# A decoder block on Trainium2: all SiLUs ahead of the exponentials at the turn from projection to scan, the first relus on VectorE, and the thin passes in small sets

## The reference, cut to what matters

```python
z, xBC, dt_raw = split(layernorm(x) @ in_proj_w.T)          # 512, 640, 8 columns
xBC = silu(causal_conv4(xBC) + conv_b)                      # xs 512, B 64, C 64
dt  = softplus(dt_raw + dt_bias); dA = exp(dt * -exp(A_log))
h_t = h_(t-1) * dA_t + (dt_t * xs_t) B_t ;  y_t = h_t C_t   # 8 heads of 64, state 64
y   = rms((y + D * xs) * silu(z)) * ssm_norm_w @ out_proj_w.T
# then an MLP; then the mLSTM, whose gates are
gates = [q, k, v] @ gate_w + gate_b                         # k = v = ctx, 8 columns
```

## Time and profile before

| | us |
|---|---|
| median of 3 runs | 598.36 (597.4 to 600.65) |
| the profiled execution, its own time | 597.5 |
| its span, first to last instruction | 595.8 |
| TensorE busy | 563.0 (94%) |
| VectorE busy | 446.2 (75%) |
| ScalarE busy | 270.1 (45%) |
| GpSimd busy | 145.7 (24%) |

### The profile page before, as it was taken

How to read it: one execution, slowest core, us unless ns; L and a number is a source line. 1 busy time by engine, 2 the same in 40 slices (tenths; PEclk the granted TensorE clock), 3 DMA queues, 4 the chain that set the end, 5 groups by cost and what they waited for, 6 DMA issues and landing times. The chain is left out here.

```text
span 595.8 us, 9377 instructions
## 1 busy us (share of the span) xinstructions
PE 563.0 (94%) x2995; PEld 457.9 (77%) x2995; DVE 446.2 (75%) x990; ACT 270.1 (45%) x565; POOL 145.7 (24%) x209
## 2 busy tenths in 40 slices
PE   6989989999999899999999999999968999999995
PEld 5767666788898788888888888878854677777774
DVE  6996797399897324765755856587888999999994
ACT  2666778776787412311111112445524445444431
POOL 4130010144454121210110010007765122222200
PEclk9999999799999999999999999999958999999998
DMA  8300001000000092000000000011000000000000
GB/s 287 141 2 25 28 17 57 3 26 7 7 4 1 28 295 72 1 1 0 1 1 1 1 0 1 4 38 56 18 2 0 1 19 18 18 17 9 18 19 26
DMA packets 21392, 18.90 MB, mean 32 GB/s; under 512 B 12008, under 2 KB 20584, under 8 KB 20968
## 3 DMA queue, kind: packets, MB, share of 16 engines
q1 hardware_dynamic: 20920, 18.36, 9.7%
q10 hardware_dynamic: 432, 0.03, 0.1%
HBM read 16.04 MB, written 2.34 MB: 31 GB/s over the span
## 5 line engine op out<-in xcount | busy, mean ns | idle before, releaser
L926 PE MATMUL ps<-xnT,w_fc 128*128 128x256 f32 x512 | 112.8, 380 | 0.0
L926 PEld LDWEIGHTS ps<-xnT,w_fc 128*128 128x128 f32 x512 | 96.5, 190 | 12.7
L1662 PE MATMUL ps<-w_fc,scores 128*128 128x352 f32 x256 | 82.9, 479 | 2.4 <-ACT scores L1751 2.4
L1662 PEld LDWEIGHTS ps<-w_fc,scores 128*128 128x128 f32 x256 | 49.3, 198 | 30.1 <-ACT scores L1751 4.3
L1169 ACT ACTIVATE xs<-ps 128x512 f32<-128x512 f32 x32 | 19.1, 597 | 95.8 <-PE ps L926 75.7
L1282 DVE SCALAR_TENSOR_TENSOR fold<-xpad,conv_w,fold 128x256 f32<-128x256 f32 x120 | 50.9, 482 | 2.4 <-ACT fold L1071 1.6
L1681 PE MATMUL ps<-u_res,hT 128*128 128x256 f32 x192 | 45.9, 391 | 3.8 <-DVE scores L1860 2.8
L1681 PEld LDWEIGHTS ps<-u_res,hT 128*128 128x128 f32 x192 | 37.5, 196 | 11.8 <-issue 3.0
L809 PE MATMUL ps<-xnT,fold 128*128 128x256 f32 x160 | 37.7, 381 | 1.4 <-ACT xpad L1065 0.9
L809 PEld LDWEIGHTS ps<-xnT,fold 128*128 128x128 f32 x160 | 29.5, 190 | 8.4 <-issue 3.0
L735 POOL TENSOR_SCALAR q_ve<-q_mv 128x2 f32<-128x2 f32 x8 | 1.7, 218 | 129.3 <-DVE q_mv L1396 129.3
(11 more groups left out here) (299 smaller groups left out, 1207.4 us busy)
## 6 DMA issues: line engine op xcount, KB each, us to landing
zs<-in_ffn_w SPq DMA_DIRECT2D x1, 2112.0 KB, 11.1
x_res<-in_x SPq DMA_DIRECT2D x8, 256.0 KB, 7.9
w_fc<-in_w_fc SPq DMA_DIRECT2D x1, 2048.0 KB, 10.3
xnT<-in_ctxT SPq DMA_DIRECT2D x8, 256.0 KB, 3.1
xs<-in_ctx SPq DMA_DIRECT2D x16, 128.0 KB, 2.9
xs<-in_ctxT SPq DMA_DIRECT2D x8, 256.0 KB, 3.1
out<-scores SPq DMA_DIRECT2D x16, 128.0 KB, 1.7
fold<-in_w_in SPq DMA_DIRECT2D x2, 580.0 KB, 6.8
```

What stands on the lines that cost most here:

```text
L926: last = pe.matmul(bank[half + r][:, i * S:(i + 1) * S], m.w_fc1[:, kk, col:col + P], m.xnT[:, b, kk * S:(kk + 1) * S], start=(kk == 0), s ...
L1662: last = pe.matmul(bank[1 + j][:, 0:HALF], xT[:, p, k * P:(k + 1) * P], m.w_gu[:, k, j * HALF:(j + 1) * HALF], start=(k == 0), stop=(k == ...
```

## The change

1. **Taps.** ScalarE does the first tap of batches 0, 1 and 2 (`TAPPED = (0, 1, 2)`) instead of 6 and 7.
2. **Time passes.** `time_steps(j)` becomes `time_step(n)`, one tile at a time; the four of a step are put between other passes. `soft_start` waits for all 16.
3. **z passes first.** In steps 3 and 4 both z passes come before the next transposes (`ROWS_FIRST`).
4. **Context sums.** `ctx_sums` takes one batch: batches 0 to 4 in steps 5 to 9, batches 5 and 6 in step 10. One counter serves the context loads, each of which waits for the one before it.
5. **The turn.** On TensorE the z passes of batch 7 follow the two decay tiles of batch 0 one by one, and its second transpose of xs goes behind the first two `mix`. On ScalarE all SiLUs, those of z of batch 7 among them, come before the decay exponentials, and the exponentials of batches 0 and 1 follow. The four relus of batch 0 are done by VectorE (`first_exponents`).

```diff
...
     SCAN, MLP = 9, 18
     STEPS = MLP + B + 3
     PAD = CONV - 1
-    TAPPED = 6
+    TAPPED = (0, 1, 2)
+    ROWS_FIRST = (3, 4)
+    conv_steps = lambda b: sum(NCH * (PAD - 1 if i in TAPPED else PAD) for i in range(b))
+    taps_before = lambda b: NCH * sum(1 for i in TAPPED if i < b)
     ORDER = [4, 0, 1, 2, 3]
     PAIRS = KM // 2
     flat = lambda t: t.rearrange("p t h -> p (t h)")
...
     PAIR_OF_ONES = 1.0 + 0x3F80 * 2.0 ** -23
     PAIR_OF_MINUS_ONES = -(1.0 + 0xBF80 * 2.0 ** -23)
     CTX_SUMS = B - 1
-    CTX_FIRST = 3
+    CTX_STEP = 5
     CTX_AT = 3 * P
 
 
...
 
         def load_ctx(b):
             sp.wait_ge(s["z_ps"], C * (b + 1))
+            after(sp, g["ctx_in"], 16 * b)
             sp.dma_start(m.xnT[:, b, :].rearrange("p (k t) -> p k t", k=KD), m.a["ctxT"][:, :, b * S:(b + 1) * S])\
-              .then_inc(g["ctx_in0"] if b < CTX_FIRST else g["ctx_in1"] if b < CTX_SUMS else g["ctx_in2"], 16)
+              .then_inc(g["ctx_in"], 16)
 
         for b in range(4):
             load_ctx(b)
...
         def turned_u(b, kk):
             return m.xnT[:, b, kk * S:(kk + 1) * S]
 
-        def time_steps(j):
+        def time_step(n):
             pe.wait_ge(s["w_in_in"], 16 * KD)
-            pe.wait_ge(s["uT_ready"], 2 * j + 2)
-            for n in range(4 * j, 4 * j + 4):
-                for kk in range(KD):
-                    last = pe.matmul(bank[7][:, n * NH:(n + 1) * NH],
-                                     turned_u(n // C, kk)[:, (n % C) * P:(n % C + 1) * P],
-                                     w_in[:, kk, DIN - NH:DIN], start=(kk == 0), stop=(kk == KD - 1))
+            pe.wait_ge(s["uT_ready"], n // C + 1)
+            for kk in range(KD):
+                last = pe.matmul(bank[7][:, n * NH:(n + 1) * NH],
+                                 turned_u(n // C, kk)[:, (n % C) * P:(n % C + 1) * P],
+                                 w_in[:, kk, DIN - NH:DIN], start=(kk == 0), stop=(kk == KD - 1))
             last.then_inc(s["dt_ps"], 1)
 
         def sum_steps():
...
                 last = pe.transpose(bank[5][:, k * P:(k + 1) * P], xF[:, b % 2, k, c * P:(c + 1) * P], m.ident[:])
             last.then_inc(s["xsT_ps"], 1)
 
-        def ctx_sums(first, end, arrived):
-            pe.wait_ge(g[arrived], 16 * (end - first))
+        def ctx_sums(b, saved):
+            pe.wait_ge(g["ctx_in"], 16 * (b + 1))
             pe.wait_ge(s["weights_summed"], 1)
-            pe.wait_ge(s["g_saved"], B - 1)
-            for b in range(first, end):
-                for c in range(C):
-                    at = CTX_AT + (C * b + c) * 2 * XH
-                    for k in range(KD):
-                        pe.matmul(bank[6][:, at:at + 2 * XH], m.xnT[:, b, k * S + c * P:k * S + (c + 1) * P],
-                                  m.gate_kv[:, k, :], start=(k == 0), stop=(k == KD - 1))
+            pe.wait_ge(s["g_saved"], saved)
+            for c in range(C):
+                at = CTX_AT + (C * b + c) * 2 * XH
+                for k in range(KD):
+                    pe.matmul(bank[6][:, at:at + 2 * XH], m.xnT[:, b, k * S + c * P:k * S + (c + 1) * P],
+                              m.gate_kv[:, k, :], start=(k == 0), stop=(k == KD - 1))
 
         def ctx_sums_last():
-            pe.wait_ge(g["ctx_in2"], 16)
+            pe.wait_ge(g["ctx_in"], 16 * B)
             pe.wait_ge(s["decays_kept"], 1)
             for c in range(C):
                 for k in range(KD):
...
         for k in range(STEPS):
             b = k - SCAN
             if k < SCAN + 1:
+                tiles = range(4 * (k - 2), 4 * (k - 1)) if 2 <= k < 6 else None
                 on(channels, k - 2, [0, 1, 2])
-                if k == 3:
-                    rows(0, 0)
-                    rows(0, 1)
+                if tiles:
+                    time_step(tiles[0])
+                if k in ROWS_FIRST:
+                    rows(k - 3, 0)
+                    time_step(tiles[1])
+                    rows(k - 3, 1)
+                    time_step(tiles[2])
                 on(turn_u, 2 * k - 2)
-                if k > 3:
+                if k not in ROWS_FIRST:
                     on(rows, k - 3, 0)
+                    if tiles:
+                        time_step(tiles[1])
                 on(channels, k - 2, [3, 4])
+                if tiles and k not in ROWS_FIRST:
+                    time_step(tiles[2])
+                if k >= CTX_STEP:
+                    ctx_sums(k - CTX_STEP, k - 3)
                 on(score, k - 3)
                 on(turn_u, 2 * k - 1)
                 on(turn_x, k - 3, 0)
-                on(time_steps, k - 2, n=4)
                 if k == 7:
                     sum_steps()
-                if k > 3:
+                if k not in ROWS_FIRST:
                     on(rows, k - 3, 1)
+                if tiles:
+                    time_step(tiles[3])
                 on(turn_x, k - 3, 1)
                 on(decays, b, 0)
                 if b == 0:
-                    ctx_sums(0, CTX_FIRST, "ctx_in0")
+                    rows(B - 1, 0)
                 on(decays, b, 1)
                 continue
             if k == SCAN + 1:
-                rows(B - 1, 0)
-                ctx_sums(CTX_FIRST, CTX_SUMS, "ctx_in1")
+                rows(B - 1, 1)
+                ctx_sums(CTX_SUMS - 2, B - 1)
+                turn_x(B - 1, 0)
+                ctx_sums(CTX_SUMS - 1, B - 1)
                 score(B - 1)
-                turn_x(B - 1, 0)
-                rows(B - 1, 1)
-                turn_x(B - 1, 1)
             on(fc1, k - MLP, 0)
             on(fc1, k - MLP, 1)
             on(turn, b - 2, 0)
...
             on(project_out, b - 2, 0)
             on(decays, b, 1)
             on(mix, b - 1, 1)
+            if k == SCAN + 1:
+                turn_x(B - 1, 1)
             on(project_out, b - 2, 1)
             if b == 3:
                 ctx_sums_last()
...
         def first_tap(b, k):
             n, ch = NCH * b + k, ORDER[k]
             act.wait_ge(s["xpad_ready"], n + 1)
-            act.wait_ge(s["silu_ready"], NCH * (b - 1))
+            after(act, s["silu_ready"], NCH * (b - 1))
             act.activation(conv[:, b % 2, k, :], xpad[:, b % 2, k, 0:S], ACT.Copy, scale=m.conv_w[:, ch, 0:1])\
                .then_inc(s["tap_ready"], 1)
 
...
             if b == 1:
                 act.wait_ge(s["z_ps"], T)
             after(act, s["y_ps"], n - 3)
-            for half in range(2):
+            for half in range(2 if b else 0):
                 act.wait_ge(s["seg_ps"], 2 * n + half + 1)
                 act.activation(E[b % 2][c][:, 512 * half:512 * (half + 1)], bank[half][:], ACT.Relu, scale=-1.0)\
                    .then_inc(s["seg_read"], 1)
...
                 on(turned_xn, b - 6)
             for i in range(3):
                 on(pad, k - 2, i)
-                on(first_tap, k - 2 if k - 2 >= TAPPED else B, i)
+                on(first_tap, k - 2 if k - 2 in TAPPED else B, i)
                 on(silu, k - 3, i)
             on(turned, 2 * k - 2)
             on(silu_z, k - 3, 0)
             for i in range(3, NCH):
                 on(pad, k - 2, i)
-                on(first_tap, k - 2 if k - 2 >= TAPPED else B, i)
+                on(first_tap, k - 2 if k - 2 in TAPPED else B, i)
                 on(silu, k - 3, i)
+            if k == SCAN + 1:
+                silu_z(B - 1, 1)
+                ends()
+                exps(0, 0)
+                exps(0, 1)
+                save_x(B - 1, 0)
+                save_scores(B - 1)
+                exps(1, 0)
+                save_x(B - 1, 1)
+                exps(1, 1)
+                continue
             on(save_scores, k - 3)
             on(turned, 2 * k - 1)
             on(save_x, k - 3, 0)
...
             on(silu_z, k - 3, 1)
             on(save_x, k - 3, 1)
             if b == 0:
-                ends()
+                continue
             on(silu_gate, k - MLP, 0)
             on(silu_gate, k - MLP, 1)
             on(squares, b - 2, 0)
...
             for tap in range(CONV):
                 for k in tiles:
                     n, ch = NCH * b + k, ORDER[k]
-                    if tap == 0 and b >= TAPPED:
+                    if tap == 0 and b in TAPPED:
                         dve.wait_ge(s["xpad_ready"], n + 1)
-                        dve.wait_ge(s["tap_ready"], n + 1 - NCH * TAPPED)
+                        dve.wait_ge(s["tap_ready"], taps_before(b) + k + 1)
                         continue
                     if tap == 0:
                         dve.wait_ge(s["xpad_ready"], n + 1)
                         dve.tensor_scalar(conv[:, p, k, :], xpad[:, p, k, 0:S], m.conv_w[:, ch, 0:1], None,
                                           ALU.mult).then_inc(s["conv_step"], 1)
                         continue
-                    if b < TAPPED:
-                        before = PAD * (NCH * b + tiles[0]) + len(tiles) * (tap - 1) + (k - tiles[0]) + 1
-                    else:
```

(21 more changed lines are left out.)

2 lines of the change are left out of this document (1 added, 1 removed).

## The result

| | before | changed |
|---|---|---|
| median of 20 runs, us | 600.01 (597.4 to 604.47) | 596.89 (593.97 to 600.35) |
| the profiled execution, its own time | 597.5 | 594.4 |
| its span | 595.8 | 592.6 |
| TensorE / VectorE / ScalarE busy | 563.0 / 446.2 / 270.1 | 564.0 / 446.9 / 267.3 |

The ratio is 0.9939, 95% interval 0.9919 to 0.996: faster by 0.6%, some 3.7 us, where 1.2% was forecast. The median of the changed kernel, 596.89, lies just outside the range of 588 to 596. The kernel before has 600.01 as the median of 20 runs, where three runs had given 598.36; its profiled execution, 597.5, is close to the fastest of the 20.

The account below looks back on a forecast made before the run. TensorE was taken to bound the kernel, alone at the turn. Terms -4.7 - 3.1 + 0.9 + 0.3 + 0 = -6.6 us from the profiled 597.5 gave 590.9, predicted as 591.0; 8-in-10 range 588 to 596.

Parts of the forecast that it names:

- The turn up to the first product, -4.7, -3.1 and +0.9: Projection to scan: 40 thin passes moved away -4.7, full clock -3.1 us, first product waiting on the SiLU-to-weighting chain +0.9.
- The clock, -3.1: At the turn, passes in the half-clock stretch from 110 to 117 us would run at 2.4 GHz: -3.1 us.
- the clock falls all the same: Rival at the turn: thin sets, scores and wait still stand close together; 3.1 us comes back, 594.1; chance 0.15.
- The rule of the Trainium skill: At the turn: if only idle gaps lower the clock, spreading thin passes saves nothing there; sum 3.1 us less good.
- Drain of the table load: ScalarE at the turn: load taken as 1.28 us without drain; the skill's 2.66 would make the chain 1.4 us longer.
- The relus on VectorE, nothing on the path: Batch 0's four first relus, 2.2 to 2.8 us in all, lie where VectorE idled at the turn: no cost.
- Later waits, +0.3: Early scan: waits for ScalarE's copies, relus and exponential mostly covered by TensorE's first products; +0.3 us, between 0 and 1.2.
- The projection, 0: Steps before the turn: added thin sets +4.7 us, offset by closed holes; net taken as 0, ends -1.7 and +3.

Follow-up runs that it names:

- the kernel that waits 2.81 us: Changed kernel with the context sums of batches 5 and 6 moved from the turn into the scan behind batch 3: 600.08 us, ratio 0.9982.
- the kernel with the clock held: Changed kernel with three unused 256-column passes on TensorE in the wait before the first product: 591.25 us, ratio 0.9844.

## Why the prediction was wrong

- **Where the miss comes from.** Of the 5.9 us between the forecast of 591.0 and the median, 596.89, some 2.4 lie in the starting point: the forecast was made from the profiled execution's 597.5 (and rounded up by 0.1), and the kernel before has a median of 600.01. The other 3.5 lie in the gain, 3.1 us instead of 6.6.
- **The turn up to the first product, -4.7, -3.1 and +0.9: right.** From the start of the turn to the first product it is 9.25 us instead of 16.41, by the rows: 7.2 less, of which 0.44 is the transpose that only moved. The passes that had stood at half clock, the z pass of 3.34 among them, do run at full clock. The wait is 1.17 us (0.9 forecast), its releaser the weighting on VectorE, as the chain said.
- **The clock, -3.1: the step that failed.** The prediction took the fall at 110 to belong to the long run of thin passes alone, and let it go with them. It stayed, and took other passes: with two thin sets, a wait and products of 64 columns behind it the clock was at half for some 10 us instead of 7, which cost 4.8 us, by the kernel with wide passes. So what was gained ahead of the first product was lost behind it. The kernels with the wait filled show that the wait has to do with it (wide passes there keep 1.00, passes of 8 columns do not). Why thin passes act like a wait stays open. The rival *the clock falls all the same* (0.15) came true in its mechanism; its price of 3.1 was too small, since it was that of a fall of 7 us.
- The argument against that rival, that products of 64 columns run at 1.00 through the scan, was no test of the turn: in the scan they stand between projections of 256 columns, at the turn behind thin sets and a wait.
- **The rule of the Trainium skill** (TensorE: Matmul & The Clock Gate, "Why this matters for your kernels") that idle gaps bring the clock down agrees with the kernel that waits 2.81 us. The gaps that the page names are longer than the waits of 0.9 and 1.17 us, so by the page this fall was not to be expected, though the prediction reads the rule that way. As the only cause it disagrees with the run of thin passes at 137.14 and with the wait filled by thin passes, both without idle time.
- **Drain of the table load:** the next activation starts at 106.93, 1.30 us behind the load's start. The trace's price was the right one, as the start of the first product shows.
- **The relus on VectorE, nothing on the path: right**, at 0.64 each, within the bounds. That they are also worth some 1 to 3 us against ScalarE was not costed.
- **Later waits, +0.3: low.** Between the first product and the scan's first transposes the kernel with the clock held takes 6.35 us, before it was 4.93: 1.4 more. Of it 0.44 is the moved transpose, which the sum rightly left out; 1.0 stands against the 0.3, most of it the wait of 0.78 for that transpose's copy.
- **The projection, 0: some 1 us too poor.** In the profiled execution step 10 starts 1.2 us earlier, at 100.38. But in eight executions with this same projection it starts anywhere from 100.31 to 101.81, and in two with the projection of before at 101.54 and 102.81. The sum has no term for the clock in the projection: four of the five executions that wait at 36 us have a fall behind that wait, which the changed order takes away.
- **The sum holds once the clock is held, in part by luck.** With the wide passes the profiled span is 588.6 and 589.0, where the prediction had 590.9 - 1.7 = 589.2. Up to the first pass of the MLP these two are 6.2 and 6.7 us ahead of the profile before (189.92 and 189.40 against 196.09), where 6.6 was forecast. In that the projection is 0.2 and 0.7 better than the sum has it, and the later waits are 0.7 longer.

## What to carry to other kernels

In this kernel the stretch at half clock did not go away with the passes that ran in it: it took what stood there next, here the first products of the scan. When a change shortens the work ahead of a wait, or leaves thin passes beside one, look at the granted clock there first, and try wide passes of no use in the wait before moving anything else. In a stretch that TensorE itself sets such passes cost their own time, and in the kernel before they gained nothing. And an edit that looks good alone (spreading the thin sets) can be a loss, here because the passes taken away had covered a wait for a relu behind a table load, and because the place that they went to had no room for them.

## What the runs showed of the hardware that was not expected

- 1.3 us of TensorE work whose result nobody reads lowers the time by 5.6 us; 1.4 us of passes with 8 columns in the same place changes nothing (596.92 against 596.89).
- With TensorE busy in each us, the clock fell behind 24 passes of 8 columns (2.74 us at 137.14), while the same number at 101.99 before left it at 1.00 for the next 5 us.
- Behind a wait of 2.3 to 2.8 us in the projection TensorE ran at half clock for some 3 us in four profiled executions, and in a fifth, with a wait of 2.43 us, it did not.
- Executions of one kernel differ by 6 us with their mean granted clock: of the changed kernel, eight of 20 have 0.974 and 594.0 to 594.8 us, four 0.960 and 599.7 to 600.4. What places a fall in one execution and not in another was left open.
